# Value batches of 6, 5 and 6 rounds in place of 4, 4, 4 and 5, in an attention that one plan orders on all engines

## What is computed

```python
R_hat = (1.0 + jnp.exp(vv)) / (1.0 + jnp.exp(vv - wv * R))          # R = |i - j|
scores = jax.nn.relu(jnp.einsum('bhqd,bhkd->bhqk', q, k)) * R_hat[None]
scores = jnp.where(causal[None, None], -jnp.inf, scores)
attn = jax.nn.softmax(scores / np.sqrt(hd).astype(x.dtype), axis=-1)
ctx = jnp.einsum('bhqk,bhkd->bhqd', attn, val)
```

## Time and profile before

| | us |
|---|---|
| median of the runs | 1583.41 |
| the runs | 1582.59 to 1583.48 |
| profiled execution, its time | 1579.39 |
| profiled execution, its span | 1577.2 |
| busy in the span: TensorE matmul | 1459.4 (93%) |
| TensorE weight load | 1142.2 (72%) |
| VectorE | 1194.4 (76%) |
| ScalarE | 1080.2 (68%) |
| GpSimd | 906.8 (57%) |

### The profile page before, as it was taken

How to read it: one execution, slowest core, us unless ns; L and a number is a source line. 1 busy time by engine, 2 the same in 40 slices (tenths; PEclk the granted TensorE clock), 3 DMA queues, 4 the chain that set the end, 5 groups by cost and what they waited for, 6 DMA issues and landing times. The chain is left out here.

```text
span 1577.2 us, 43271 instructions
## 1 busy us (share of the span) xinstructions
PE 1459.4 (93%) x15923; PEld 1142.2 (72%) x16142; DVE 1194.4 (76%) x3650; ACT 1080.2 (68%) x2069; POOL 906.8 (57%) x1510
## 2 busy tenths in 40 slices
PE   6894999999999999999899999999997758999997
PEld 4551788888888888888788888888886546666675
DVE  6643999999999999999799999999976694223222
ACT  3443888898889888998788988898884770211211
POOL 3332777677767777777677777677773001324322
PEclk9997899999999999999999999999999856999999
DMA  6334222322232222223223222322234333334532
GB/s 219 121 118 147 70 64 63 91 72 67 61 91 75 67 62 78 83 71 109 66 67 94 71 64 63 92 74 65 88 126 142 93 114 122 99 95 98 153 74 24
DMA packets 90030, 142.44 MB, mean 90 GB/s; under 512 B 18032, under 2 KB 69632, under 8 KB 85728
## 3 DMA queue, kind: packets, MB, share of 16 engines
q1 hardware_dynamic: 82058, 128.70, 26.4%
q0 software_dynamic: 6464, 9.29, 3.2%
q10 hardware_dynamic: 1302, 1.74, 0.3%
HBM read 109.56 MB, written 30.15 MB: 89 GB/s over the span
## 5 line engine op out<-in xcount | busy, mean ns | idle before, releaser
L834 ACT ACTIVATE region_o<-turn_ps 128x512 f32<-128x512 f32 x576 | 347.5, 615 | 53.1 <-PE turn_ps L799 45.5
L788 PE MATMUL score_ps<-region_s 128*128 128x384 bf16 (+3 forms) x1061 | 347.3, 348 | 12.0 <-DVE maxima L867 4.9
L834 ACT ACTIVATE region_p<-turn_ps 128x512 f32<-128x512 f32 x512 | 304.7, 612 | 75.6 <-PE turn_ps L799 75.4
L799 PE MATMUL turn_ps<-ident,region_a 128*128 128x128 f32 x2048 | 335.6, 275 | 16.0 <-ACT region_o L834 4.8
L799 PE MATMUL turn_ps<-ident,region_x 128*128 128x128 f32 x2048 | 336.5, 274 | 1.7
L799 PEld LDWEIGHTS turn_ps<-ident,region_a 128*128 128x128 f32 x2048 | 260.0, 141 | 51.5 <-ACT region_o L834 13.6
L902 POOL TENSOR_SCALAR region_x<-region_x,maxima 128x1664 f32<-128x1664 f32 (+3 forms) x128 | 211.3, 1651 | 143.9 <-ACT region_x L839 140.7
L867 DVE CUSTOM_DVE_ANT_0 region_x<-score_ps,region_t,maxima 128x512 f32<-128x512 f32 (+1 forms) x416 | 272.2, 700 | 11.7 <-PE score_ps L788 10.6
L799 PEld LDWEIGHTS turn_ps<-ident,region_x 128*128 128x128 f32 x2048 | 254.4, 141 | 34.4 <-issue 6.5
L867 DVE CUSTOM_DVE_ANT_0 region_a<-score_ps,region_t,maxima 128x512 f32<-128x512 f32 (+1 forms) x352 | 231.4, 697 | 24.5 <-PE score_ps L788 22.9
L839 ACT ACTIVATE region_x<-region_x 128x512 f32<-128x512 f32 (+1 forms) x320 | 218.7, 684 | 4.5 <-DVE maxima L867 4.5
(11 more groups left out here) (215 smaller groups left out, 2163.3 us busy)
## 6 DMA issues: line engine op xcount, KB each, us to landing
region_t<-factor_rows SPq DMA_DIRECT2D x32, 1024.0 KB
region_x<-in_fc_t SPq DMA_DIRECT2D x16, 1024.0 KB, 8.5
region_s<-q_split SPq DMA_DIRECT2D x64, 192.0 KB
region_s<-k_split SPq DMA_DIRECT2D x64, 192.0 KB
q_split<-region_o SPq DMA_DIRECT2D x16, 384.0 KB, 2.7
k_split<-region_t SPq DMA_DIRECT2D x16, 384.0 KB, 2.6
heads_out<-region_o SPq DMA_DIRECT2D x254, 17.0 KB
region_x<-in_x SPq DMA_DIRECT2D x4, 1024.0 KB, 15.2
```

The costliest lines, as they stand in the source:

```text
L788: nc.tensor.matmul(score_ps[:, j % SB, 0:(hi - lo) * P], stacks[:, b, 0, t * P:(t + 1) * P], stacks[:, b, 1, lo * P:hi * P], start=True, s ...
L799: last = nc.tensor.transpose(turn_ps[:, (h * NR + j) % TB, q * P:(q + 1) * P], rows[t][:, k * P:(k + 1) * P], ident[:, :])
L834: nc.scalar.activation(weight(j), turn_ps[:, (h * NR + j) % TB, :], ACT.Exp).then_inc(exp_done, 1)
```

## The change

- A group's values are taken in three batches of 6, 5 and 6 rounds in place of four of 4, 4, 4 and 5. Even and odd batches have six weight slots each: to the nine in `region_p` and `region_o` come slots in the upper half of `region_c`, of which three are used.
- `region_c`'s upper half is therefore not free for finished heads during attention: at head 8 four loads are issued in place of eight, and after attention eight in place of four.
- The plan's clock: a batch takes `PV_START + PV_ROUND` x its rounds, and transposes are spaced by what is left (`pace`). Batches, saves, dumps and what follows them are placed by this clock.
- TensorE's part of a score and VectorE's become two events, TensorE's 2.5 rounds (`AHEAD`) before VectorE's. `LEAD` is 19 for 20.
- ScalarE's ReLU is cut into pieces of at most three blocks for five, planned at least 0.8 rounds apart for 1.2, and tile 8 is clamped by GpSimd.

```diff
-    BATCHES = (4, 4, 4, 5)
+    BATCHES = (6, 5, 6)
     NBT = GROUPS * len(BATCHES)
     TB = 3
-    LEAD = 20
-    PV_LAG = 3.2
+    LEAD = 19
+    PV_AFTER, PV_ROUND, PV_START, AHEAD = 3, 0.232, 0.26, 2.5
...
     weight_slots = [region_p[:, i * SW:(i + 1) * SW] for i in range(4)] + [region_o[:, i * SW:(i + 1) * SW] for i in range(5)]
+    weight_slots += [region_c[:, 4096 + i * SW:4096 + (i + 1) * SW] for i in range(8)]
...
-    RELU_ON_ACT = (15, 13, 12, 11, 9, 8)
-    SHIFT_BLOCKS, RELU_BLOCKS, RELU_GAP = 7, 5, 1.2
+    RELU_ON_ACT = (15, 13, 12, 11, 9)
+    SHIFT_BLOCKS, RELU_BLOCKS, RELU_GAP = 7, 3, 0.8
...
     def weight(r):
-        return weight_slots[in_batch[r] + (4 if batch_of[r] % 2 else 0)]
+        return weight_slots[in_batch[r] + (max(BATCHES[0::2]) if batch_of[r] % 2 else 0)]
+
+
+    pv_time = [PV_START + PV_ROUND * BATCHES[k % len(BATCHES)] for k in range(NBT)]
+    pv_place = [(batch_end[k] + PV_AFTER) % NR for k in range(NBT)]
+    pace = (NR - sum(pv_time)) / NR
+
+    def at_round(r):
+        heads, r = divmod(r, NR)
+        return heads * NR + pace * r + sum(t for t, place in zip(pv_time, pv_place) if place < r)
+
+    pv_at = [at_round(batch_end[k] + PV_AFTER) + 0.5 * pace for k in range(NBT)]
+
+    def saved_at(g):
+        return pv_at[(g + 1) * len(BATCHES) - 1] + pv_time[(g + 1) * len(BATCHES) - 1] + 0.3
...
-    events = [(float(r), "turn", r) for r in range(NR)]
-    events += [(due[s], "score", s) for s in range(NS)]
-    events += [(batch_end[k] + PV_LAG, "pv", k) for k in range(NBT)]
-    events += [((g + 1) * ROUNDS - 1 + PV_LAG + 0.9, "save", g) for g in range(GROUPS)]
-    events += [((g + 1) * ROUNDS - 1 + PV_LAG + 1.4, "dump", g) for g in range(GROUPS)]
+    events = [(at_round(r), "turn", r) for r in range(NR)]
+    events += [(due[s], "scale", s) for s in range(NS)]
+    events += [(due[s] - AHEAD, "score", s) for s in range(NS)]
+    events += [(pv_at[k], "pv", k) for k in range(NBT)]
+    events += [(saved_at(g), "save", g) for g in range(GROUPS)]
+    events += [(saved_at(g) + 0.5, "dump", g) for g in range(GROUPS)]
     events += [(due[last_of[b]] + 1, "load", b) for b in range(B)]
-    gathered_at = [NR // B * (b + 1) - 1 + PV_LAG + 4 for b in range(B)]
+    gathered_at = [saved_at(GROUPS // B * (b + 1) - 1) + 3 for b in range(B)]
...
-                        for g in range(NG):
+                        for g in range(NG // B):
                             load_heads(sp, g, 0)
...
-                if what == "score":
+                if what == "scale":
...
             for g in range(GB, G):
-                load_heads(sp, g, 1)
+                for k in range(KC):
+                    load_heads(sp, g, k)
             spread_inverse(sp, H - 1, B - 1)
```

More of the change, by code:

```diff
@@ L544, in attention @@
 def attention(nc, o):
-    region_x, region_a, region_o, region_p = (o[k] for k in ("region_x", "region_a", "region_o", "region_p"))
+    region_x, region_a, region_o, region_p, region_c = (o[k] for k in ("region_x", "region_a", "region_o", "region_p", "region_c"))
     x, vals, ident, add_bias, dump = o["x"], o["vals"], o["ident"], o["add_bias"], o["dump"]
@@ L675, in attention @@
     events += [(gathered_at[b] + 12, "spread", b) for b in range(B)]
-    events += [(NR // B * (b + 1) - 1 + PV_LAG + 1.1 - NR, "values", b) for b in range(B)]
+    events += [(saved_at(GROUPS // B * (b + 1) - 1) + 0.2 - NR, "values", b) for b in range(B)]
     relu_due, at = [0.0] * len(relu_parts), -NR
@@ L706, in attention @@
     for n, (b, t) in enumerate(tiles):
-        assert due[slots_of[n][0]] > last_round(t) - NR // B + b * NR // B + 1
+        assert due[slots_of[n][0]] > at_round(last_round(t) - NR // B + b * NR // B) + 0.6, (n, due[slots_of[n][0]], at_round(last_round(t) - NR // B + b * NR // B))
         group = (0 if t in firsts[0] + seconds[0] else 1) + 2 * b
         need = group * ROUNDS + (0 if t in firsts[0] + firsts[1] else ROUNDS - t - 1)
-        assert ready[n] + 3.5 < need, (n, b, t, ready[n], need)
+        assert ready[n] + 3.5 < at_round(need), (n, b, t, ready[n], at_round(need))
     with ExitStack() as st, nc.Block() as block:
```

## The result

The kernel after takes 1566.62 us, median of six runs (1563.45 to 1569.96), against 1582.61 for the kernel before in six runs beside it (1581.21 to 1583.48). The ratio is 0.99, with a 95% interval of 0.9886 to 0.9913. That is the predicted 1566.6 us; that it agrees to the tenth is luck, since the runs themselves spread over 6.5 us and errors cancel in the sum. The profiled execution took 1563.45 us, with a span of 1561.4; the sum had said 1562.6.

A forecast was written before the change was run, and what follows sets the result against it. TensorE's stream was taken to set attention's period. From the profiled 1579.4 us, -13.6 - 6.6 + 1.4 + 2.0 gave 1562.6; with the run median 4.0 above that execution, the forecast was 1566.6 us, range 1560 to 1573.

The forecast's parts named there:

- Fewer batches: In attention, 62 fewer value batches at 0.22 us each on TensorE: -13.6 us.
- Rival D: In attention, batches are no cheaper, their cost returning as other waits: 1580 us, chance 0.07.
- Longer batches at no cost: In attention, ScalarE draws on finished turns during 1.54 us without transposes and has idle time: cost 0.
- Order of the queues and ReLU at no gain or cost: In attention's steady part, the new queue order, smaller ReLU pieces and tile 8 on GpSimd cost 0.
- My two zeros: In attention's steady part, cost 0 for longer batches and 0 for the new queue order with the ReLU edits.
- Rivals A and B: In attention, VectorE's holds reach TensorE (A, about 1610 us, chance 0.15); ScalarE holds the transposes (B, 1573 us, 0.14).
- The stall at head 8: At head 8, four loads for eight free SyncE's queue before the dumps: -6.6 us, bounds 0 and 6.66.
- The start of attention: At attention's start, first transpose 1.8 us late, three more scores (0.45 us) done by then: +1.4 us.
- Loads after attention: After attention, four more loads go ahead of the inverted sums: +2.0 us, range 0 to 5.2.

The follow-up runs named there:

- clock_only: The kernel after with the old batches of 4, 4, 4 and 5 rounds; 1579.76 us, 0.9983 of the kernel before.
- batches_only: The kernel before with the moved loads of heads, batches of 6, 5 and 6 and their slots, under the old plan; 1595.71 us, ratio 1.0083.
- loads_only: The kernel before with only the loads of heads moved: four for eight at head 8, eight for four after attention; 1583.70 us, ratio 1.0003.
- one_by_one: slots_high with its six early loads issued singly, two in each of heads 8, 9 and 10; 1560.39 us, 0.9856 of the kernel before.
- no_ahead: The kernel after with TensorE's part of a score no longer ahead of VectorE's (AHEAD 0); 1588.78 us, 1.0040 of the kernel before.
- slots_high: The kernel after with three slots at region_c's end, two more loads at head 9, two loads ahead of the inverses after attention; 1556.01 us, 0.9872 of before.
- split_loads: The kernel before with its eight loads at head 8 split, four there and four at head 9; 1570.17 us, ratio 0.9955.
- second set: Four kernels on a chip of their own, varying the loads and the plan, beside the kernel before at a median of 1577.34 us.
- third: Set on another chip: each ReLU edit undone alone, batches untimed in the clock, early loads issued singly; the kernel before had a median of 1582.66 us.
- first set: Four kernels on one chip, separating loads, batches, clock and scores ahead; the kernel before had a median of 1582.74 us.
- no_pace: The kernel after with a plan's clock in which a batch takes no time (PV_ROUND and PV_START 0); 1602.49 us, 1.0124 of the kernel before.
- relu_old: The kernel after with the old ReLU: five-block pieces, gap 1.2, tile 8 on ScalarE; 1588.35 us, 1.0073 of the kernel before.

## Why the prediction was right, and where its steps were not

**Fewer batches: mechanism right, size nearly.** 0.19 us a batch for 0.22. A six-round batch leaves the same remainder of 0.13 us. Rival D (batches no cheaper) is refuted by clock_only against the kernel after.

**Longer batches at no cost: this step failed as it was argued.** I had said that ScalarE draws on finished turns while a batch runs, and that it has idle time enough. batches_only shows that it doesn't: its transposes wait 3.7 us a head, and the longer batches cost 0.41 us a half head net. I had counted ScalarE's 3.7 us of idle time in a half head as spare. But 3.5 of them (7.0 a head) were already waits for transposes, so they couldn't take up work that has to follow the transposes.

**Order of the queues and ReLU at no gain or cost: failed too.** The plan's edits are what makes the batches pay. From 32.36 to 31.43 us they bring 0.93 a half head. Taken back alone from the kernel after, the pacing costs 1.15, the small pieces 0.82, the scores ahead 0.70 and tile 8 0.47. They overlap, so they don't sum. `LEAD` was never varied by itself. My two zeros were wrong by +0.85 (0.41 against -0.44) and -0.93 a half head, and it was their sum that was near zero: a half head is 31.43 where I had 31.51. Rivals A and B were both real mechanisms, each behind an edit that keeps it away. In the kernel after, neither decides (2.4 us of waits for VectorE, below the 3 that I had named, and 1.1 for ScalarE, below 2). That the chances of 0.15 and 0.14 were well set is more than one result can say.

**The stall at head 8: right.** The term was -6.6 us. loads_only removes all 6.66, and the kernel after keeps 1.14, so -5.5; one_by_one shows that these were still the four loads in one go.

**The start of attention: wrong sign.** The first transpose comes at 163.25, 1.1 us late for the 1.8 that I had. Attention itself starts at another time in each execution, with its first score between 144.2 and 148.2 us in the fourteen traces. Counted from that score, the first transpose is 1.6 us late (17.87 us for 16.29), and without the scores ahead it comes 2.5 us earlier (no_ahead, 15.32). So this half of the term was right. But already the fourth set of transposes starts at 166.39, for 166.45 before, and at the second save the kernel is 1.8 us ahead; for that place my terms say 1.0 behind (+1.4, less 0.44 for two batches). Counted from the first score it is 1.3 us ahead (52.38 for 53.70); slots_high and one_by_one, which have the same plan, are 0.8 and 0.7 ahead. The granted clock doesn't settle why. Windows of the kernel after, from 160 to 172:

```profile
160.00:166.00 6.00, 5.35 (x21) 3.16 (x22) 6.00 (x22) 3.73 (x6) 4.63 (x10) 0.57 0.16 65
166.00:172.00 6.00, 6.00 (x85) 4.98 (x83) 5.79 (x20) 5.57 (x13) 5.47 (x15) 1.00 0.03 12
```

The mean granted clock is 0.57 and 1.00 of 2.4 GHz, for 0.50 and 0.97 before in the same windows. That is 6 x 0.07 + 6 x 0.03 = 0.6 us at the full clock. But from 140 to 160 it is 0.62 for 0.73, which is 2.2 us the other way. The cause stays open.

**Loads after attention: mis-sized, +6.4 us for +2.0**, and above my upper bound of 5.2. I had priced the transfer and given it 3.5 us of slack. What it delays, by these rows, is the small transfer of the inverses, on which all loads of inverses wait: 8.5 us for 3.6 in the kernel after, 9.5 in loads_only, 1.4 in slots_high with two loads ahead. On one chip the tail's excess is 5.3 to 6.9 us over slots_high, and 5.7 to 7.3 over split_loads. It lies between the start of the projection and the first count of the router, 69.1 and 70.8 us for 62.5 and 62.8. In the profile of the kernel after this stretch accounts for 3.1 of the 6.4 (67.6 for 64.5). The others are +0.7 ahead of it, +1.7 up to the first GELU and +0.9 behind. The +1.7 may well be no cost of the change: this stretch is 83.1 to 84.0 us in all four kernels of the second set and 89.2 and 89.7 in two of the third, whatever their loads. One profiled tail is also known only to some 5 us, as the first set shows. Taken as a whole, the move of the loads (-6.6 and +2.0 in my sum) gained nothing in loads_only, so the 16 us of the result are the work of the batches and the plan, for which my sum had 12.2.

The Trainium skill, DMA: Bandwidth & Descriptors, Specifications, whose 358 GB/s would by my estimate have made the added megabyte 2.9 us and free, lies further from these rows than my own term: four loads more made the wait behind the spread 4.9 us longer. The 120 GB/s that I set beside it is only the rate at which the queue took the eight loads. In the same 17.5 us the DMA engines moved 170 GB/s, with other transfers under way.

So the total is right to 0.1% and two errors cancel in it: in the profiled execution attention came out 3.4 us better than the sum had it, and the tail 4.4 us worse.

## What to carry to other kernels

A fixed cost of every switch between two kinds of work on the bounding engine can be saved by longer runs of each, but the engines that feed on the work between starve and can then hold it. Idle time of such an engine is no reserve when it is a wait for that very work. Measure the longer run and the new interleaving as a square of four kernels, since either alone may lose. A plan of several queues needs a clock that counts the bounding engine's long stretches. Put few bulk loads ahead of a small transfer on which others wait, and spread bulk loads where dumps of the same queue feed a wait.

## What the runs showed of the hardware

**The price of an issue on SyncE.** A load of 256 KB held the queue for 2.18 us when four or eight stood together at head 8 (8.72 and 17.50 us), but 0.67 us each for eight after attention (5.32 us). The eight dumps behind them took 2.03 us each (16.27 us), and single loads in one_by_one 1.6 to 4.6, so this isn't a matter of the loads. **A small transfer behind bulk.** The spread of the inverses was in memory after 1.4 us behind two such loads, 3.6 behind four, and 8.5 to 9.5 behind eight; the kernel with two also has fewer loads in all. **Shifts of VectorE.** One shape took from 560 ns (batches_only) to 1421 (no_pace) on average, with no difference in its own work. The Trainium skill, SBUF — State Buffer, Who interferes with whom, names a shared port that locks VectorE or GpSimd out for a whole instruction, and the traces agree: the shift of 1.65 us in relu_old ended 0.35 us after the GpSimd subtraction in which it began, for 0.54 us without one. **Chips.** With the half head equal to the hundredth, the kernel before took 1577.3 us on one chip and 1582.7 on two others; the kernels with after's loads have tails of 414 to 416 us on the first and 419 to 424 on the others.
